# Two-layer attention kernel: the order of GpSimd's work on the output tiles, four places for tile statistics, weights loaded by SyncE, x tiles in one transfer

## The reference, cut to what matters

```python
x = L0_attn_x                                     # (2, 1024, 512) float32
x = x + layernorm(attn0(layernorm(x)))            # 32 heads of 16, no mask
x = x + layernorm(ffn0(layernorm(x)))             # gate/up/down, integer weights, 1376 wide
x = x + layernorm(attn1(layernorm(x)))            # one k/v head, ALiBi, causal
x = x + layernorm(ffn1(layernorm(x)))             # z = xW'+b, m = low-rank, z + gamma*m
```

## Time and profile before

| | before |
|---|---|
| median of 3 runs (lowest, highest) | 2093.04 us (2090.45, 2093.83) |
| the profiled execution's own time | 2097.88 us |
| its span | 2096.1 us |
| busy PE / PEld | 92% / 52% |
| busy DVE / ACT / POOL | 67% / 55% / 12% |
| mean granted PE clock | 0.97 |
| tail loops, layer 0 / layer 1 | about 873 to 938 us / 1926 to 1986 us |

### The profile page before, as it was taken

How to read it: one execution, slowest core, us unless ns; L and a number is a source line. 1 busy time by engine, 2 the same in 40 slices (tenths; PEclk the granted TensorE clock), 3 DMA queues, 4 the chain that set the end, 5 groups by cost and what they waited for, 6 DMA issues and landing times. The chain is left out here.

```text
span 2096.1 us, 31854 instructions
## 1 busy us (share of the span) xinstructions
PE 1923.5 (92%) x11664; PEld 1088.5 (52%) x11664; DVE 1403.7 (67%) x2438; ACT 1162.4 (55%) x2422; POOL 242.1 (12%) x305
## 2 busy tenths in 40 slices
PE   6999999999999999879999998499999999999684
PEld 4865333333333333458888887364444444444463
DVE  5346999999999998444334232467777877773567
ACT  3224888888788888544222221224777777774453
POOL 0000000110000000341011010100002000003413
PEclk9999999999999999989999999697999999999898
DMA  6582544355434530323010000472544443322101
GB/s 206 158 191 75 78 77 93 63 83 82 78 62 82 77 74 22 96 87 97 1 40 21 21 21 0 146 176 64 97 100 83 99 94 77 77 62 72 47 21 60
DMA packets 118636, 165.60 MB, mean 79 GB/s; under 512 B 48372, under 2 KB 52852, under 8 KB 118336
## 3 DMA queue, kind: packets, MB, share of 16 engines
q1 hardware_dynamic: 112256, 142.28, 31.1%
q0 software_dynamic: 6224, 21.29, 3.2%
HBM read 104.92 MB, written 58.06 MB: 78 GB/s over the span
## 5 line engine op out<-in xcount | busy, mean ns | idle before, releaser
L959 DVE TENSOR_REDUCE maxesB<-banksB 128x1 f32<-128x1024 f32 x512 | 601.9, 1215 | 85.6 <-PE banksB L1028 85.4
L909 ACT ACTIVATE probsB<-banksB 128x512 f32<-128x512 f32 x1024 | 529.5, 603 | 127.6 <-PE banksB L1039 127.4
L956 DVE CUSTOM_DVE_ANT_0 junkG<-banksG,rampG 128x896 bf16<-128x896 f32 (+7 forms) x512 | 368.2, 756 | 106.5 <-PE banksG L1028 99.4
L1039 PE MATMUL banksB<-q_stackB,k_stackB 50*128 50x512 f32 x1024 | 403.6, 471 | 4.1 <-ACT probsB L909 2.1
L909 ACT ACTIVATE probsG<-banksG 128x512 f32<-128x512 f32 (+3 forms) x768 | 326.1, 492 | 120.2 <-PE banksG L1050 66.6
L1028 PE MATMUL banksB<-k_stackB,q_stackB 48*128 48x512 f32 x1024 | 344.1, 441 | 3.9
L1039 PEld LDWEIGHTS banksB<-q_stackB,k_stackB 50*128 50x128 f32 x1024 | 166.6, 184 | 264.6 <-ACT probsB L909 232.6
L1039 PE MATMUL banksG<-q_stackG,k_stackG 54*128 54x512 f32 (+3 forms) x768 | 262.8, 419 | 20.9 <-ACT probsG L909 16.0
L1072 PE MATMUL banksB<-probsB,v_onesB 128*32 128x512 f32 x2048 | 273.5, 606 | 0.0
L1028 PE MATMUL banksG<-k_stackG,q_stackG 52*128 52x512 f32 (+3 forms) x768 | 251.4, 415 | 8.0 <-DVE maxesG L956 7.9
L1028 PEld LDWEIGHTS banksB<-k_stackB,q_stackB 48*128 48x128 f32 x1024 | 153.7, 185 | 85.8 <-DVE maxesB L959 75.1
(11 more groups left out here) (301 smaller groups left out, 2808.7 us busy)
## 6 DMA issues: line engine op xcount, KB each, us to landing
q_stackB<-q_parts SPq DMA_DIRECT2D x96, 128.0 KB
k_stackB<-k_parts SPq DMA_DIRECT2D x96, 128.0 KB
q_stackG<-q_parts SPq DMA_DIRECT2D x96, 128.0 KB
q_parts<-partsA SPq DMA_DIRECT2D x16, 512.0 KB, 4.0
k_parts<-partsA SPq DMA_DIRECT2D x16, 512.0 KB, 2.8
turns<-o_copyB SPq DMA_DIRECT2D x32, 256.0 KB, 2.2
q_parts<-partsF SPq DMA_DIRECT2D x16, 512.0 KB, 2.8
turns<-o_copyG SPq DMA_DIRECT2D x32, 256.0 KB, 3.1
```

The source lines that it names most:

```text
L909: act.activation(probs[:, (i % ring) * GH + h, first:HALF], st_ps[:, n % n_st, first:HALF], ACT.Exp).then_inc(st_used, 1)
L956: dve.tensor_tensor_reduce(junk[:, n % JUNK, 0:width], scores, ramp[:, SEQ - width:SEQ], 1.0, LOWEST, ALU.add, ALU.max, out).then_inc(maxe ...
L959: dve.reduce_max(out, scores, AX.X).then_inc(maxed, 1)
L1039: ins = pe.matmul(st_ps[:, n % n_st, first:HALF], kst[at, it % 3, h % kh, kt * P:(kt + 1) * P], qst[at, it % 3, half, h % GS, first:HALF], ...
```

## The change

1. POOL's tail loop does root(t) ahead of add(t - 1); the last add follows the loop.
2. Statistics, mean, root and shift get four places (t % 4), and waits on "normed" go from t - 2 to t - 4.
3. DVE's tail loop does `tile_shift(t - 1)` always ahead of `tile_low(t + 2)`.
4. `load_rest` is one transfer of 2 MB with no wait.
5. All of `Gated`'s weight pieces are issued by SP: 0 and 1 inside attention, 2 to 20 in `sync`, after the wait for the last `spread_inverse`. `load_first` of `Gated` is empty; `Adapter`'s stays with POOL.
6. The stores of blocks 2 and 3 of x go from SP to POOL (`keep`): at t = 13 and after the tail loop.
7. `Adapter.tensor` waits for the 16 normed tiles only after its first product u.

```diff
@@ SP, in the loop over attention
+                if it >= 10:
+                    nxt.load_early(sp, it - 10)
@@ POOL, in the loop over attention
-                    if it >= 10:
-                        nxt.load_early(pool, it - 10)
@@ POOL, tail loop
             for t in range(tiles_ahead, NT):
+                out.tile_root(pool, t)
                 if t == tiles_ahead + 4:
                     divide(last)
-                out.tile_root(pool, t)
-                out.tile_add(pool, t)
+                if t > tiles_ahead:
+                    out.tile_add(pool, t - 1)
                 nxt.gpsimd_tile(pool, t, out)
-            nxt.gpsimd(pool)
+            out.tile_add(pool, NT - 1)
+            nxt.gpsimd(pool, out)
@@ DVE, tail loop
                 out.tile_stats(dve, t, s_ps)
-                if t + 2 < NT and t + 2 != NT - TB:
-                    out.tile_low(dve, t + 2)
                 if t > tiles_ahead:
                     out.tile_shift(dve, t - 1)
-                if t + 2 == NT - TB:
+                if t + 2 < NT:
                     out.tile_low(dve, t + 2)
@@ Output.load_rest
-        for nb in range(self.SLOTS // TB, NB):
-            if nb > self.SLOTS // TB:
-                engine.wait_ge(*self.x_in(TB * nb - 1))
-            engine.dma_start(self.block(nb), self.x[BLK * nb:BLK * (nb + 1), :].rearrange("(t p) d -> p t d", p=P)
-                             ).then_inc(self.x_loaded, 16)
+        engine.dma_start(self.xu[:, :, :], self.x[P * self.SLOTS:, :].rearrange("(t p) d -> p t d", p=P)
+                         ).then_inc(self.x_loaded, 16)
@@ Output.tile_stats (the places of mv, rstd and shift likewise)
-        if t >= 2:
-            dve.wait_ge(self.normed, t - 1)
-        dve.bn_aggr(self.mv[:, t % 2, :], self.stats[:, t % 2, :]).then_inc(self.meaned, 1)
+        if t >= 4:
+            dve.wait_ge(self.normed, t - 3)
+        dve.bn_aggr(self.mv[:, t % 4, :], self.stats[:, t % 4, :]).then_inc(self.meaned, 1)
@@ Output.tile_root
-        if t >= 2:
-            pool.wait_ge(self.normed, t - 1)
+        if t >= 4:
+            pool.wait_ge(self.normed, t - 3)
@@ Gated
     def load_first(self, pool):
-        for i in range(2, 4):
-            self.load_piece(pool, i)
+        pass
+    def keep(self, pool, nb, out):
+        pool.wait_ge(out.added, TB * (nb + 1))
+        if nb > 2:
+            pool.wait_ge(self.kept, 16 * (nb - 2))
+        pool.dma_start(self.x[BLK * nb:BLK * (nb + 1), :].rearrange("(t p) d -> p t d", p=P), out.block(nb)
+                       ).then_inc(self.kept, 16)
     def gpsimd_tile(self, pool, t, out):
-        if t == 11:
-            self.load_piece(pool, 4)
-            self.load_piece(pool, 5)
         if t == 13:
-            self.load_piece(pool, 6)
-            self.load_piece(pool, 7)
+            self.keep(pool, 2, out)
     def sync(self, sp, out):
-        for nb in range(2, NB):
-            sp.wait_ge(out.added, TB * (nb + 1))
...
+        for i in range(2, len(self.pieces)):
+            self.load_piece(sp, i)
-    def gpsimd(self, pool):
-        for i in range(8, len(self.pieces)):
-            self.load_piece(pool, i)
+    def gpsimd(self, pool, out):
+        self.keep(pool, 3, out)
@@ Adapter.tensor
-        pe.wait_ge(out.normed, NT)
...
             if nb == 0:
                 pe.wait_ge(w.ready, w.count("bm"))
+                pe.wait_ge(out.normed, NT)
```

More of the change, by code:

```diff
@@ L1146, in __init__ @@
         self.onl = sb(f"onlT{tag}", [P, 3, DC, P], F32R)
[L1147 to L1150, removed]
+        self.stats = sb(f"ystats{tag}", [P, 4, 6], F32)
+        self.mv = sb(f"ymv{tag}", [P, 4, 2], F32)
+        self.rstd = sb(f"yrstd{tag}", [P, 4], F32)
+        self.shift = sb(f"yshift{tag}", [P, 4], F32)
         self.yn = sb(f"yn{tag}", [P, 2, D], F32)
@@ L1157, in x_in @@
     def x_in(self, t):
-        return (self.x_first, 16 * (t + 1)) if t < self.SLOTS else (self.x_loaded, 16 * ((t - self.SLOTS) // TB + 1))
+        return (self.x_first, 16 * (t + 1)) if t < self.SLOTS else (self.x_loaded, 16)
     def tile(self, t):
@@ L1212, in tile_stats @@
         dve.wait_ge(self.made, t + 1)
[L1213 removed]
+        dve.bn_stats(self.stats[:, t % 4, :], y_ps[:, t % 4, :]).then_inc(self.summed, 1)
         dve.wait_ge(self.summed, t + 1)
[L1215 to L1217 removed]
+        if t >= 4:
+            dve.wait_ge(self.normed, t - 3)
+        dve.bn_aggr(self.mv[:, t % 4, :], self.stats[:, t % 4, :]).then_inc(self.meaned, 1)
         dve.wait_ge(self.meaned, t + 1)
[L1219 removed]
+        dve.tensor_scalar(self.mv[:, t % 4, 1:2], self.mv[:, t % 4, 1:2], LN_EPS, None, ALU.add).then_inc(self.padded, 1)
     def tile_norm(self, dve, t, y_ps):
@@ L1224, in tile_norm @@
             dve.wait_ge(self.added, t - 1)
-        dve.tensor_scalar(self.yn[:, t % 2, :], y_ps[:, t % 4, :], self.mv[:, t % 2, 0:1],
-                          self.rstd[:, t % 2:t % 2 + 1], ALU.subtract, ALU.mult).then_inc(self.normed, 1)
+        dve.tensor_scalar(self.yn[:, t % 2, :], y_ps[:, t % 4, :], self.mv[:, t % 4, 0:1],
+                          self.rstd[:, t % 4:t % 4 + 1], ALU.subtract, ALU.mult).then_inc(self.normed, 1)
     def tile_shift(self, dve, t):
         dve.wait_ge(self.rooted, t + 1)
-        dve.scalar_tensor_tensor(out=self.shift[:, t % 2:t % 2 + 1], in0=self.mv[:, t % 2, 0:1], scalar=-1.0,
-                                 in1=self.rstd[:, t % 2:t % 2 + 1], op0=ALU.mult, op1=ALU.mult).then_inc(self.shifted, 1)
+        dve.scalar_tensor_tensor(out=self.shift[:, t % 4:t % 4 + 1], in0=self.mv[:, t % 4, 0:1], scalar=-1.0,
+                                 in1=self.rstd[:, t % 4:t % 4 + 1], op0=ALU.mult, op1=ALU.mult).then_inc(self.shifted, 1)
     def tile_scale(self, act, t, y_ps):
@@ L1236, in tile_scale @@
         act.wait_ge(self.added, t - 1)
-        act.activation(self.yn[:, t % 2, :], y_ps[:, t % 4, :], ACT.Identity, bias=self.shift[:, t % 2:t % 2 + 1],
-                       scale=self.rstd[:, t % 2:t % 2 + 1]).then_inc(self.normed, 1)
+        act.activation(self.yn[:, t % 2, :], y_ps[:, t % 4, :], ACT.Identity, bias=self.shift[:, t % 4:t % 4 + 1],
+                       scale=self.rstd[:, t % 4:t % 4 + 1]).then_inc(self.normed, 1)
     def tile_root(self, pool, t):
         pool.wait_ge(self.padded, t + 1)
-        if t >= 2:
-            pool.wait_ge(self.normed, t - 1)
-        pool.tensor_tensor(self.rstd[:, t % 2:t % 2 + 1], self.mv[:, t % 2, 1:2], self.power[:, 0:1], ALU.pow
+        if t >= 4:
+            pool.wait_ge(self.normed, t - 3)
+        pool.tensor_tensor(self.rstd[:, t % 4:t % 4 + 1], self.mv[:, t % 4, 1:2], self.power[:, 0:1], ALU.pow
                            ).then_inc(self.rooted, 1)
@@ L1400, in landed_piece, with load_piece @@
         return self.landing(i).rearrange("p m (j f) -> p j m f", j=columns) if columns else self.landing(i)
-    def load_piece(self, pool, i):
+    def load_piece(self, sp, i):
         if i >= 4:
-            pool.wait_ge(self.w_low, i - 3)
-        pool.dma_start(self.landing(i), self.pieces[i][0]).then_inc(self.landed[i % 4], 16)
+            sp.wait_ge(self.w_low, i - 3)
+        sp.dma_start(self.landing(i), self.pieces[i][0]).then_inc(self.landed[i % 4], 16)
     def high(self, act, which):
@@ L1448, in sync @@
         n, r = self.n, self.r
-        def rows(dram, nb):
-            return dram[BLK * nb:BLK * (nb + 1), :].rearrange("(t p) d -> p t d", p=P)
-        for nb in range(2, NB):
-            sp.wait_ge(out.added, TB * (nb + 1))
-            if nb > 2:
-                sp.wait_ge(self.kept, 16 * (nb - 2))
-            sp.dma_start(rows(self.x, nb), out.block(nb)).then_inc(self.kept, 16)
+        for i in range(2, len(self.pieces)):
+            self.load_piece(sp, i)
         for nb in range(NB - 1):
@@ L1464, in sync @@
                 sp.wait_ge(r.stored, 16 * (nb + 1))
-                sp.dma_start(n.block(nb + 2), rows(self.x, nb + 2)).then_inc(n.loaded, 16)
+                sp.dma_start(n.block(nb + 2), self.x[BLK * (nb + 2):BLK * (nb + 3), :].rearrange("(t p) d -> p t d", p=P)
+                             ).then_inc(n.loaded, 16)
         store_last(sp, r, n, self.x_out)
-    def gpsimd(self, pool):
-        for i in range(8, len(self.pieces)):
-            self.load_piece(pool, i)
+    def gpsimd(self, pool, out):
+        self.keep(pool, 3, out)
         for nb in range(NB):
@@ L1625, in weights_low, with load_early @@
         self.w.split_low(dve, [self.w.order[k]])
-    def load_early(self, pool, k):
+    def load_early(self, sp, k):
         pass
```

4 lines of the change are left out of this document (2 added, 2 removed).

## The result

The changed kernel took 2068.12 us (median of 4 runs, 2061.47 to 2075.12) beside 2093.43 for the kernel before on the same chip: a ratio of 0.9877 with a 95% interval of 0.9848 to 0.9906. That is 25.7 us less on 2093 (20 to 32), where 30.9 were forecast. The runs with the higher times also had the lower mean clock of PE (0.970 and 0.971 for 2075, 0.979 and 0.978 for 2061).

A forecast was written before the change was run, and what follows sets the result against it. With PE busy 92% of the span, only its standstills in both layers' tails could give much. Gains of 16.6 (layer 0) and 14.3 (layer 1), together 30.9, off 2093.04 gave 2062.1 us; range 2050 to 2069.

The forecast's parts named there:

- First gap, layer 0: PE's wait for normed tiles after tile 7: 6.4 us to become 3.8, transposes 2.7 us earlier.
- First gap, layer 1: PE's wait for normed tiles after tile 7: 8.6 us to become 6, transposes 2.65 us earlier.
- my upper end: Latest landing of layer 1's last sums, at 1942; 1940 was taken, with 1935.3 as the early bound.
- the release: POOL's go-ahead after layer 1's first MB of x, taken to come some 2 us after the last byte.
- The tail chain: Tile 8 to the next block, root and addition no longer alternating on POOL: 11.1 us in layer 0, 8.85 in layer 1.
- the clock behind it: PE's clock no longer at half speed after the last gap: 2.8 us in each layer.
- the last gap of layer 0: PE's 9.6 us wait for the first silu at the tail's end, put down to POOL's alternation; forecast to vanish.
- Queues take turns: Rival, chance 0.22: q1 gets its turn inside the 2 MB, sums land as before, clock stays up; 2051 us.
- what q0 has been given goes ahead of q1: Reading of both tails' transfers: the second MB of x delays layer 0's sums by 2.8 us, to 885.2.
- A new chain holds the tail: Rival, chance 0.09: DVE's list with its waits for ACT grows to 3.5 us and more per tile; 2080 us.
- Weights late: Rival, chance 0.03: weight pieces sharing q1 land late, PE waits in 8 steps of the first block; 2102 us.
- The order changes nothing: Rival, chance 0.02: the gaps stay because the last inverses rule them; 2092 us.

The follow-up runs named there:

- only_order: Kernel before with only root ahead of the last tile's addition, four places for statistics and shift ahead of low part: 2068.03 us, ratio 0.9877.
- weights_pool: Changed kernel with Gated's weight pieces issued by POOL and the stores of x by SP, as before: 2069.92 us, ratio 0.9897.
- u_waits: Changed kernel with PE again waiting for all normed tiles ahead of layer 1's u: 2069.89 us, ratio 0.9899.
- the repetition: The changed kernel run again without any edit, for the spread of stage numbers: 2068.91 us, ratio 0.9887.
- x_q0_late: Changed kernel with x and Adapter's weights issued by POOL behind tile 4's root and a wait for the last sums: 2060.39 us, ratio 0.9851.
- both_late: Changed kernel with x and Adapter's weights issued by SP behind the sums' fetch, and DVE's reciprocal behind tile 7's statistics: 2055.84 us, ratio 0.984.

## Why the prediction was right, and where it was off

**The number.** Forecast was 2062.1, measured 2068.12, inside the stated 2050 to 2069 but 1.1 above the forecast's own range of 2057 to 2067. That it stays inside is in part luck: the four runs were 2061.5, 2061.7, 2074.6 and 2075.1, and the median lies between the pairs. The stages are the better test.

**First gap, layer 0.** As forecast, POOL's wait went, the root of tile 4 ran at 877.50 (forecast about 877.5), and the wait for the last sums took its place. In layer 0 they landed at 885.6 (forecast 885.2), PE waited 4.1 us (3.8), and the transposes gained 2.35 (2.7).

**First gap, layer 1: the term that was mis-sized.** I put the sums at 1940, which is 14.0 us after the tail's first matmul; they came 17.5 after it (1918.38 - 1900.86). PE waited 9.3 us instead of 6, and the transposes, forecast 2.65 us earlier, came 0.7 later. Against the forecast the transposes are 3.3 us late, and even my upper end, 1942, was too early. The working gave 1935.6 for the first MB and 8 us for the other 2.5 MB, so 1943.6, or 17.6 after the first matmul, close to what came; I then took 2 us off for the release, which gave the upper end, and 2 more for no measured reason. The rate was off too: q0's 3.67 MB moved from about 1903.3 to 1917.7, 0.25 MB per us, not the 0.32 of 1937 to 1943.1. The sums, issued at 1904.37, came 0.7 us behind the last of it.

**The tail chain.** Layer 0: forecast 2.7 + 11.1 before the second product, and 2.8 for the clock behind it; measured 13.7 and 2.8, so 16.5 against 16.6. The silu was done before the up product, as forecast. In layer 1 from the transposes on: 45.7 us became 33.7, a gain of 12.0, where the terms 8.85 and 2.8 give 11.65. That they agree is partly luck: from tile 8 to u the gain was 9.8 (forecast 8.85), from u to the first z product 1.45 (forecast 2.8, with no wait for tile 15's scale, which was 0.8), and transposes with tile 8, left at 6.0 in the forecast, took 5.3 instead of 6.1. Layer 1 in all: 11.4 against 14.3. **The sum** is 27.9 against 30.9, and the 3.0 missing come from the mis-sized landing.

**One cause was missed.** Part of the last gap of layer 0 was no alternation on POOL. ACT's timeline of the kernel before has a wait for a weight piece that POOL had issued at 919.07, behind an addition:

```profile
925.45 0.63 ACT L1410 ACTIVATE wd0D<-landD 128x512 fp32r<-128x512 int32 x1 [3.39 <-DMA landD<-in_down_w]
```

With the order alone that wait is gone too (ACT has none for a DMA in `only_order` and `weights_pool`), as POOL comes to the issue earlier. Handing the weights to SP was then not needed for it.

**What each part is worth.** The forecast gave the one transfer 2.7 + 2.65 and the order the rest. This is the step that failed. The runs show: the transfer alone gains nothing (1.0018); in the changed kernel it costs, by the stages of one profile, 2.3 to 3.6 us per layer against two transfers; the order alone has 0.9877, though it lacks the step ahead of u, worth 5 us in layer 1 (`u_waits` against the repetition). The two nearly cancel. The forecast's sum held because it followed the whole change to what was late next; its split by parts did not, since POOL's wait and the one for the sums end close together and each hides the other. Within the order, the shift's place is 2.3 to 3.7 us per layer and the four places about 1 at most; the root's place ahead of the addition, which is left with the rest, was not run alone.

**The rivals.** *Queues take turns*: not as the rival has it, since the sums landed at 885.6 and not at 882.4. But the forecast's reading, that what q0 has been given goes ahead of q1, is only half right too. In layer 0 the DMA view has no packet of q1 from 876.2 to 880.2, though SP issued from 876.11 on, and from 880.2 to 884.5 it has (packets, MB, share):

```profile
q0 software_dynamic: 245, 0.94, 66.0%
q1 hardware_dynamic: 501, 0.32, 27.8%
```

So q1 moved while nearly half of x was still to come. Layer 1, first 1904 to 1908, then 1908 to 1913, shows the same two behaviours:

```profile
q0 software_dynamic: 282, 1.16, 93.3%
...
q0 software_dynamic: 317, 1.20, 79.3%
q1 hardware_dynamic: 211, 0.32, 23.8%
```

For the first 4 us q1 gets nothing, though SP issued four transfers between 1903.79 and 1905.89; after that it gets packets in between, and still the sums come late. Why q1 starts 4 us late in both layers is not settled. The Trainium skill's rule that was weighed against this forecast (page "DMA: Bandwidth & Descriptors", section "Queues, rings and completion order": each DMA engine goes round between its queues) agrees with the second stretch and not with the first. *A new chain holds the tail*: no, DVE's list took the time that was counted. *Weights late*: no, no piece made PE wait in the first block, and putting them back on POOL moved layer 0's second product by 0.3 to 1.2 us. *The order changes nothing*: the opposite, the order is the gain.

## What to carry to other kernels

A wait that is removed from one engine is worth only the distance to the next one that is due at the same place; look for what lands at that moment before counting it, and test each part alone. Where an engine has to wait for a small transfer, move its place in the list first: one reciprocal two tiles later gave as much as another way for 2 MB. A tiny instruction that another engine waits for goes ahead of a longer one that is needed later: the shift of 0.15 us ahead of a low part of 0.69 was worth 2.3 to 3.7 us per layer.

## What was not expected

- A transfer of 8 KB took 8.9 us to land with 2 MB ahead of it on the other queue and 14.0 with 3.5 MB, but at most 4.5 with the same 2 MB issued *behind* it on its own queue.
- A standstill of PE of nearly the same length can cost its clock or not. In layer 1 the changed kernel waits 2.65 us for a low part at 1945.60 and goes on at full speed, and so does `x_q0_late` behind 2.69 us at 1942.66; in `both_late` the wait is 2.69 too and the window behind it has 0.50:

```profile
1939.90:1943.00 3.10, 3.00 (x7) 2.43 (x8) 2.27 (x7) 2.07 (x4) 3.10 (x4) 0.50 0.03 8
```

- The clock also differs between executions far from the edit. These are the windows of the first stretch of layer 1's attention, first before, then after:

```profile
1428.00:1452.00 24.00, 22.46 (x138) 12.12 (x138) 11.94 (x44) 12.84 (x31) 1.19 (x3) 0.50 0.37 80
```

```profile
1412.00:1419.00 7.00, 5.94 (x40) 3.25 (x41) 2.92 (x17) 3.89 (x9) 0.35 (x2) 0.52 0.51 148
1428.00:1452.00 24.00, 22.85 (x218) 11.42 (x217) 18.73 (x53) 18.48 (x45) 2.31 (x5) 1.00 0.15 49
```

  The kernel before ran there at half clock for 23.9 us, the changed one for 6.8. One pair of profiles thus overstates the change by 8.5 us; the stage numbers do not.
- One transfer in place of two, with a wait less, made the kernel before slower by 0.18% (0.03 to 0.33%).
